# Softmax sums as 32-column products, four PE-summed units in the first block, and the skipped tiles' V added by VectorE

## The reference

```python
scores = einsum('bthd,bshd->bhts', q, k)          # 16 heads of 128
scores = scores * tril(ones((T, T)))              # masked scores are 0, not -inf
attn = softmax(scores / T ** 0.5, axis=-1)
out = einsum('bhts,bshd->bthd', attn, v).reshape(B, T, H * Dh) @ Wo
x = x + layernorm(out)
hdn = silu(g * gate_s) * (u * up_s)               # 5632 wide, from layernorm(x)
x = x + layernorm((hdn @ down_w.T) * down_s)
```

## Time and profile before

| | us |
|---|---|
| median of 3 runs | 3783.23 |
| lowest, highest | 3782.91, 4057.18 |
| the profiled execution | 3785.3 |
| its longest span, core 7 (odd) | 3783.8 |
| spans of the odd cores 1, 3, 5, 7 | 3778.8, 3769.3, 3779.7, 3783.8 |
| spans of the even cores 0, 2, 4, 6 | 3709.4, 3714.5, 3705.3, 3709.6 |
| busy on core 7: TensorE, VectorE, ScalarE, GpSimd | 3685.2, 1424.9, 1158.5, 173.1 |

### The profile page before, as it was taken

One profiled execution on the slowest core, in us unless ns is written; L12 is line 12 of the kernel. 1 busy time (PEld: TensorE's weight loads), 2 busy tenths in 40 slices (PEclk: granted clock), 3 DMA queues, 4 the chain that ended last, 5 costly groups with the idle time before them and its releaser, 6 DMA issues.

```text
span 3783.8 us, 50455 instructions; the slowest of 8 cores (3705.3 to 3783.8 us)
## 1 busy us (share of the span) xinstructions
PE 3685.2 (97%) x19252; PEld 1840.7 (49%) x19252; DVE 1424.9 (38%) x1860; ACT 1158.5 (31%) x1511; POOL 173.1 (5%) x235
## 2 busy tenths in 40 slices
PE   6999889999999999999999999999999999999998
PEld 3554444444454555545544444444444456645654
DVE  4641001101389999999976611102111121111112
ACT  2330000000288888888863310000010001101100
POOL 0000000000010000100000000000200001002000
PEclk9999989999999999999999999999999999999999
DMA  7534767798544335353036564554745547666665
GB/s 197 173 123 105 117 124 129 125 134 131 84 62 94 92 78 112 77 106 82 29 134 222 176 209 156 183 173 111 239 156 184 178 145 273 232 212 222 235 201 178
DMA packets 140788, 566.57 MB, mean 150 GB/s; under 512 B 38016, under 2 KB 83200, under 8 KB 111360
## 3 DMA queue, kind: packets, MB, share of 16 engines
q1 hardware_dynamic: 59520, 381.70, 29.6%
q0 software_dynamic: 11440, 125.83, 20.5%
q10 hardware_dynamic: 69584, 55.72, 4.9%
HBM read 595.73 MB, written 147.85 MB: 197 GB/s over the span
## 4 chain that ended last, share of the span: by engine, by line
PE 94%; ACT 2%; DMA 1%; issue 1%; ACTq 1%; DVE 1%; another core or an unknown queue 0%; DVEq 0%; POOL 0%; POOLq 0%; SPq 0%
PE ps L335 93%; ACT pt L369 1%; PE ps L340 1%; ACTq L331 1%; DMA xst<-x 0%; DMA indf<-ind 0%; DVE bna L361 0%; DVE zad L358 0%; ACT rz L369 0%; DMA kscr<-stg 0%; ACT xy L369 0%; DVE xy L360 0%; ACT zst L368 0%; DVE xn L359 0%
## 5 line engine op out<-in xcount | busy, mean ns | idle before, releaser
L335 PE MATMUL ps<-zt,slab 128*128 128x512 bf16 (+1 forms) x5632 | 1069.0, 353 | 6.2 <-DVE xy L360 6.2
L335 PEld LDWEIGHTS ps<-zt,slab 128*128 128x128 bf16 x5632 | 551.7, 98 | 522.4 <-issue 9.9
L369 ACT ACTIVATE pt<-ps 128x1024 bf16<-128x1024 f32 (+2 forms) x752 | 724.9, 981 | 132.9 <-PE ps L335 103.5
L358 DVE TENSOR_TENSOR zad<-zad,pt 128x1024 f32<-128x1024 f32 (+5 forms) x640 | 614.6, 975 | 59.5 <-POOL pt L364 2.9
L335 PE MATMUL ps<-dp,hall 128*128 128x512 bf16 x2332 | 504.0, 379 | 0.0
L360 DVE SCALAR_TENSOR_TENSOR hall<-ps,us_sb,sg 128x512 bf16<-128x512 f32 (+1 forms) x176 | 120.3, 684 | 902.6 <-PE ps L335 902.6
L335 PE MATMUL ps<-qh,kh 128*128 128x512 bf16 (+1 forms) x1760 | 432.4, 339 | 9.8 <-ACT qh L368 5.8
L335 PE MATMUL ps<-pt,vh 128*128 128x512 bf16 (+1 forms) x1760 | 432.3, 339 | 1.8 <-ACT pt L369 1.1
L369 ACT ACTIVATE sg<-ps,gs_sb 128x512 f32<-128x512 f32 (+1 forms) x176 | 111.2, 635 | 878.1 <-PE ps L335 878.0
L357 DVE CAST stg<-ps 128x512 bf16<-128x512 f32 (+1 forms) x136 | 89.7, 660 | 743.0 <-PE ps L335 707.4
L335 PEld LDWEIGHTS ps<-dp,hall 128*128 128x128 bf16 x2332 | 228.2, 98 | 274.9
(11 more groups left out here) (80 smaller groups left out, 1904.8 us busy)
## 6 DMA issues: line engine op xcount, KB each, us to landing
slab<-gwc SPq DMA_DIRECT2D x44, 2048.0 KB, 8.7
slab<-uwc SPq DMA_DIRECT2D x44, 2048.0 KB, 9.5
dp<-dwc SPq DMA_DIRECT2D x165, 512.0 KB, 4.8
xst<-x SPq DMA_DIRECT2D x32, 1024.0 KB, 5.8
gwc<-gw POOLq DMA_DIRECT2D x11, 2048.0 KB, 21.7
uwc<-uw POOLq DMA_DIRECT2D x11, 2048.0 KB, 19.5
dwc<-dw POOLq DMA_DIRECT2D x8, 2816.0 KB, 22.2
kh<-kscr SPq DMA_DIRECT2D x16, 1024.0 KB, 20.0
```

Of the source, the lines that this page charges most:

```text
L335: return c.r.op("tensor", lambda E: E.matmul(out, lhsT, rhs, start=start, stop=stop), waits=waits, inc="pe" if inc else None)
L358: "tt": lambda E, o, a, b, op: E.tensor_tensor(o, a, b, op),
L369: "act": lambda E, o, i, f, **kw: E.activation(o, i, f, **kw),
```

## The change

- Odd side, phase B: `npe` is 4, 4, 4, 2 instead of 2, 3, 3, 2, and `lag` is 5 for every block instead of 3. The TensorE sums of a block are no longer made unit by unit but in one burst after the block's last product with V (`zcols`): eight products with a 128 x 32 matrix of 1/32, each into one of four groups of 32 PSUM partitions, so that each group holds a quarter of the sum. VectorE adds the bank to its folded sum (`zr`), and splits that (`split`, now a few steps after `combine`); `zbc` opens the bank anew.
- Odd side: the product for the skipped tiles' V goes. 16 small products at the start of phase B give `vskip`, one value per row and query tile, and `mul` scales each tile of 128 columns by (output + vskip) x rz, 14 instructions a head instead of 4.
- Both sides: in group 1 each odd chunk of both loops makes a cast; the two casts at the group's end go. The order of the casts and their number stay.
- Both sides: `r.split()` stands before the first statistics, after the first wv load.
- Both sides: the first gate and up groups of phase C use the banks in another order: first the two that the last row tile of phase W didn't use.

```diff
-            self.npe = {18: 2, 22: 3, 26: 3, 30: 2}
-            self.lag = {18: 3, 22: 3, 26: 3, 30: 3}
+            self.npe = {18: 4, 22: 4, 26: 4, 30: 2}
+            self.cols = True
+            self.lag = {18: 5, 22: 5, 26: 5, 30: 5}
...
+    pop(c, "memset", c.ones32[:], 1.0 / 32.0)
...
+    ev_w["v0"] = dma(c, "gpsimd", "qw0", c.wres[0][:], d["wv"].ap()[0])
+    r.split()
+
     sop(c, "act", c.lva[1][:], c.eps[:], AF.Ln, waits=[ev_const])
 
-    ev_w["v0"] = dma(c, "gpsimd", "qw0", c.wres[0][:], d["wv"].ap()[0])
     def stats(t):
...
     apply(0)
-    r.split()
...
         ev_w[f"k{g}"] = dma(c, "gpsimd", "qw1", c.wres[1][:], d["wk"].ap()[g], waits=[r.mark("pe")])
         for cc in range(nch):
-            if g > 1 and cc % 2 == 1:
+            if cc % 2 == 1:
                 next_cast(c, [r.mark("pe")])
...
-            next_cast(c, [r.mark("pe")])
-            next_cast(c, [r.mark("pe")])
...
+    if sd.cols:
+
+        for h in range(H):
+            e = mm(c, bank(c, 6)[:, h * sd.n_own:(h + 1) * sd.n_own], c.vs[:, h * 128:(h + 1) * 128],
+                   c.ind[:, 0:sd.n_own], start=True, stop=True, waits=[c.ev_vs, c.ev_ind], inc=(h == H - 1))
+        ev_zbank = vop(c, "copy", c.vskip[:], bank(c, 6)[:, 0:H * sd.n_own], waits=[e] + c.ev_stores)
...
+            if not sd.cols:
+                mm(c, o[:, 0:W], c.vs[:, h * 128:(h + 1) * 128], skipped(n),
+                   start=True, stop=False, waits=w + [c.ev_vs, c.ev_ind])
...
+    def zcols(bi, us):
+
+        W = width[blocks[bi][1]]
+        parts = [(s, p[2]) for s in us for p in steps[s][4][0]]
+        assert len(parts) % 4 == 0
+        for i, (s, pc) in enumerate(parts):
+            j = i % 4
+            ev_zmm[s] = r.op("tensor", lambda E, j=j, s=s, pc=pc, i=i: E.matmul(
+                bank(c, 6)[32 * j:32 * j + 32, 0:W], c.ones32[:], c.pt[s % NPT][:, pc:pc + W],
+                start=(i < 4), stop=(i >= len(parts) - 4), tile_position=(0, 32 * j)),
+                waits=[ev_sel[s], ev_lnread[bi - 1] if bi >= 1 else ev_zbank],
+                inc="pe" if i == len(parts) - 1 or parts[i + 1][0] != s else None)
+
     def zbc(bi):
...
+    def split(bi):
+
+        W = width[blocks[bi][1]]
+        Z, e = c.zad, ev_fold[bi]
+        if sd.cols:
+            Z = c.zr
+            u = end_unit[bi]
+            e = vop(c, "tt", Z[:, 0:W], Z[:, 0:W], bank(c, 6)[:, 0:W], ALU.add, waits=[e, ev_zmm[u]])
...
+        if sd.cols:
+            for t in range(sd.blocks[n][1]):
+                x = h * sd.n_own + sd.blocks[n][0] - sd.own[0] + t
+                q = slice(t * 128, (t + 1) * 128)
+                ev_mul[bi] = vop(c, "stt", c.aall[:, a0 + t * 128:a0 + (t + 1) * 128],
+                                 bank(c, 4 + bi % 2)[:, q], c.vskip[:, x:x + 1], c.rz[:, q], ALU.add, ALU.mult,
+                                 waits=[ev_rz[bi], ev_last_pv[bi], c.ev_a_pe, ev_zbank])
+            return
...
+    plain = ([0, 1, 2, 3], [4, 5, 6, 7])
+    last = [c.ring(L, ds) for ds in range(4)]
+    free = [b for b in range(6) if b not in last]
+    first_banks = (free + last[:2], last[2:] + [6, 7])
```

More of the change, by code:

```diff
@@ L897, in pv @@
         o = bank(c, 4 + bi % 2)
+        w = []
         if k == 0:
             w = [ev_mul[bi - 2]] if bi >= 2 else [c.ev_ln1[1]]
-            mm(c, o[:, 0:W], c.vs[:, h * 128:(h + 1) * 128], skipped(n),
-               start=True, stop=False, waits=w + [c.ev_vs, c.ev_ind])
+            if not sd.cols:
+                mm(c, o[:, 0:W], c.vs[:, h * 128:(h + 1) * 128], skipped(n),
+                   start=True, stop=False, waits=w + [c.ev_vs, c.ev_ind])
         for m, (kt, c0, pc, pw) in enumerate(u[0]):
@@ L904, in pv @@
             ev_pvm[s] = mm(c, o[:, c0:c0 + pw], V[:, kt * 128:(kt + 1) * 128], P[:, pc:pc + pw],
-                           start=False, stop=(last and fin),
-                           waits=[ev_sel[s], ev_vl[h]] if m == 0 else (), inc=fin)
+                           start=(sd.cols and k == 0 and m == 0), stop=(last and fin),
+                           waits=w + [ev_sel[s], ev_vl[h]] if m == 0 else (), inc=fin)
         if last:
@@ L936, in zbc @@
         zb = bank(c, 6)[:, 0:W]
-        mm(c, zb, c.onesb[:], c.zhi[:, 0:W], start=False, stop=False, waits=[ev_zlo[bi]])
+        mm(c, zb, c.onesb[:], c.zhi[:, 0:W], start=sd.cols, stop=False, waits=[ev_zlo[bi]])
         ev_zbc[bi] = mm(c, zb, c.onesb[:], c.zlo[:, 0:W], start=False, stop=True, inc=True)
@@ L968, in combine @@
         while half >= W:
-            e = vop(c, "tt", Z[:, 0:half], Z[:, 0:half], Z[:, half:2 * half], ALU.add,
-                    waits=[r.mark("dve")])
+            o = c.zr if sd.cols and half == W else Z
+            w = [r.mark("dve")]
+            ev_fold[bi] = vop(c, "tt", o[:, 0:half], Z[:, 0:half], Z[:, half:2 * half], ALU.add, waits=w)
             half //= 2
+    def split(bi):
[5 more added lines that the diff above has]
+            e = vop(c, "tt", Z[:, 0:W], Z[:, 0:W], bank(c, 6)[:, 0:W], ALU.add, waits=[e, ev_zmm[u]])
         w = [e] + [ev_zbc[b] for b in (bi - 1, bi - 2) if b in ev_zbc]
@@ L995, in passes @@
         return sum(p[3] for p in steps[s][4][0]) / 512.0
-    mean = (sum(2 * passes(s) + (passes(s) if by_pe(s) else 0) for s in range(per_head))
+    share = 0.25 if sd.cols else 1.0
+    end_unit = {steps[s][0]: s for s in range(N)}
+    mean = (sum(2 * passes(s) + (share * passes(s) if by_pe(s) else 0) for s in range(per_head))
             + ND * sum(nt for t0, nt in sd.blocks) / 4.0) / per_head
@@ L1027, in phase_b @@
             if by_pe(p) and not all_pe[steps[p][2]]:
-                zmm(p)
-                work += passes(p)
+                if not sd.cols:
+                    zmm(p)
+                    work += passes(p)
+                elif steps[p][5]:
+                    b = steps[p][0]
+                    us = [q for q in range(p - 8, p + 1) if q >= 0 and steps[q][0] == b and by_pe(q)]
+                    zcols(b, us)
+                    work += share * sum(passes(q) for q in us)
         for p in z_at.get(s, ()):
@@ L1053, in phase_b @@
                 combine(steps[s][0])
+                if not sd.cols:
+                    split(steps[s][0])
+        for p in pv_at.get(s, ()):
+            if sd.cols and steps[p][5]:
+                split(steps[p][0])
     while c.casts:
@@ L1197, in phase_w @@
     c.NW = NW
+    c.ring = ring
     c.ev_w_pe = ev_mm[(NW - 1, 3)]
@@ L1324, in phase_c @@
             k = 2 * (b * NIG + ig)
+            gb, ub = first_banks if b == 0 and ig == 0 else plain
             for jj in range(4):
```

27 lines of the change are left out of this document (16 added, 11 removed).

## The result

| | before | after |
|---|---|---|
| median, us | 3788.57 | 3761.38 |
| ratio, 95% interval | | 0.9939 (0.9922 to 0.9956) |
| profiled execution, longest span | 3783.8 (core 7) | 3759.8 (cores 1 and 7) |
| spans of the odd cores 1, 3, 5, 7 | 3778.8, 3769.3, 3779.7, 3783.8 | 3759.8, 3759.5, 3754.7, 3759.8 |
| spans of the even cores 0, 2, 4, 6 | 3709.4, 3714.5, 3705.3, 3709.6 | 3702.8, 3702.9, 3698.3, 3690.6 |

Two of the five executions before and one of the five after ran slower as a whole at a lower granted clock, so the ratio compares the other three and four, whose medians are 3783.23 and 3761.28 us. The change wins 0.6%, 22 to 24 us, where 50 were forecast (3733 us), and lies 1.4 us above the upper end of the range. I compare core 7 with core 7.

What follows compares the result with a forecast made beforehand. VectorE and TensorE were taken as saturated in attention, odd core 7 slowest: 3785.3 − 5 (start) − 25 (casts) − 13 (attention) − 1.5 (its end) − 6 (FFN) = 3734.8, less 2.1 to the median: 3733 us; range 3715 to 3760.

Steps and rivals of the forecast that it cites:

- Attention: Odd side's heads: period falls from 58.8 to about 58.0 us, 13 us won over 16 heads (between −17 and +5).
- Waits of TensorE for the split: Attention: a listed sign that the forecast is wrong, TensorE waiting for VectorE's split; no size given.
- don't overlap: Rival, attention: 32-column products run one after another, TensorE needs 59.0 us a head, total 3751 us; chance 0.11.
- slow bursts: Rival, attention: weight loads can't hide, bursts cost 10.0 us a head, period 62.1, total 3799 us; chance 0.07.
- VectorE alone the bound: Attention: VectorE needs 57.8 us a head against TensorE's 54.4, so it alone sets the period of about 58.0.
- The casts: Group 1, odd cores: without the burst at 411 us, TensorE's 29.9 us stop becomes 5: −25 (−5 to −30).
- The remainder of 5: Group 1: a smaller burst from 277 to about 335 us still stops TensorE 0 to 10 us, taken as 5.
- the stall moves: Rival, group 1: the stop moves rather than goes, only 7 of 29.9 us is won, total 3751 us; chance 0.12.
- The penalty of 10 us by x: Even cores: a new cast at 174 us among the loads of x costs about 10 us, net −6.
- The start: Kernel start, both sides: the earlier branch hides part of VectorE's 8.6 us idle time: −5 us (0 to 9).
- The end of attention: Odd side: add and split after the last product take some 2.2 us instead of 3.7 of waiting: −1.5.
- The FFN's first group: FFN start: two banks free early let products cover the 6.2 us wait for VectorE: −6 on odd cores, 0 on even.

Runs made afterwards that it cites:

- e1: The changed kernel with lag 3 instead of 5 for block 26 alone: 3724.2 us.
- e8: e1 with the skipped tiles' V again a TensorE product and the scaling one instruction a block: 3744.2 us.
- e5: The kernel before with only the casts changed: one at each odd chunk of group 1's V loop, the two at the group's end gone: 3746.3 us.
- e12: e1 with one cast more in group 1, at the odd chunk of its K loop, right behind Wv: 3754.8 us.
- e13: The same kernel as e12, run again for its trace: 3752.8 us (one run).
- e11: e1 with the first FFN groups using the banks in the order of before: 3727.3 us.
- e2: The changed kernel with lag 3 instead of 5 for all four blocks: 3732.1 us.

## Why the prediction was wrong

**Attention, −13 forecast, +18 measured (core 7).** This is the step that failed: "The later scaling (lag 5) costs nothing as long as VectorE is less than five units late; what is queued behind a product that waits for its split is all of TensorE." I asked only who waits for the split. The scaling has a client too, the product with V that reuses the output's bank two blocks later, and the block between is 8 units long. The bound of five units was wrong: for block 26 the scaling stands two steps ahead of that product, behind the adds and folds of block 30, and VectorE came to it 1.5 us after rz was ready. The place in the list could have been read from the code. The wait costs 15 × 1.5 = 23, and the half clock behind 9 of them 9 × 1.7 = 15, which the forecast had nowhere: e1 measures 37 together. "Waits of TensorE for the split" was named as a sign of being wrong; the scaling was not.

**The prices of the operations held.** A burst of eight 32-column products takes 0.63 us, as priced. First its row in TensorE's timeline of after (core 7), then two groups by form (count, busy us, mean ns, idle before):

```profile
1532.44 0.61 PE L959 MATMUL ps<-pt,ones 128*32 128x512 bf16 x8
```

```profile
L370 DVE SCALAR_TENSOR_TENSOR aall<-ps,vskip,rz 128x128 bf16<-128x128 f32 x224 | 63.4, 343 | 1.9 <-ACT rz L379 1.9
...
L959 PEld LDWEIGHTS ps<-pt,ones 128*32 128x32 bf16 x512 | 7.7, 94 | 23.7 <-issue 23.7
```

Four scaling pieces take 1.23 us up to the next add (1577.61 to 1578.84; priced 1.08 and 0.1 of wait), one piece 0.343 (priced 0.35), and the add of the bank 0.78 (priced 0.79). The skip products are worth 1.6 us a head (e8 against e1; priced 1.55). The rivals "don't overlap" and "slow bursts" fall. The Trainium skill's page "TensorEngine Tiling (Array Packing)", sections "Key Properties" and "Restrictions and Gotchas", has a mode switch drain the engine and fast weight load off in column tiling; here a switch costs about 0.1 us each way within the 0.63, and the loads (94 ns each) stay hidden.

**"VectorE alone the bound" was wrong, and 58.0 close by luck.** With the lag mended the period is 57.53. TensorE's work was put at 54.4 and measures 55.4: 0.6 of it because before's sum (58.0) was short of its measured 58.64 busy, and I gave the difference to waiting; the rest is open. On top come the 2.0 us of waits for ScalarE in the TensorE-summed units. VectorE was put at 57.8 and needs 55.9 (57.5 less 1.6 of waits). I took VectorE's gapless row as a need of the whole head. The wait of 0.17 us in it stands ahead of all four splits of the head, 0.7 us where I took 0.3 off; the other 1.5 us are not accounted for.

**The casts, −25 forecast, some −38 measured alone (e5).** The mechanism was right, the size wrong in three ways. The remainder of 5 rested on a cast that isn't made; the wait for Q fell too (4.6), and the end of the half clock behind both stops gave 3 to 4 us more. And had the cast been made, the price of 0 to 10 us would have been wrong as well: "a store may be some 47 us late" holds at 411, where the tile is needed 47 us after the issue. At 272 it is needed after 20 us, and the stop was 25.7. The rival "the stall moves" was the true course for the kernel that I had in mind: of 29.9 us of stop 25.7 came back. Its 3751 isn't to be set beside e12, which has e1's lag.

**Even cores.** Their stop at 371 went, as forecast. The penalty of 10 us by x doesn't exist, as the cast isn't made; the net is −7 to −19 by core, and they never decide. With the cast made the price was about right: the even cores' spans average 3708.6 us in e12 against 3700.7 in e1, and core 6 of e13 waits 10.6 us for a staging tile from 196 on, where e1 waits 2.0.

**The start, −5 forecast.** The wait for Wv fell by 5.3, but the first normed tile came 5.8 later (17.2 to 22.9 us), which the wait hid. TensorE is 2.9 us ahead at the sixth tile (62.44 against 65.33). Over all traces that tile comes at 60.2 to 64.0 us with the early branch and at 65.3 to 67.4 with the late one: within the bounds.

**The end of attention, −1.5 forecast, +2.6.** The last split and scaling wait behind lag 5 too (6.28; 4.20 in e1). **The FFN's first group, −6 forecast**, −3 by e11: its wait is gone as forecast, but the transposes of the last row tile now wait 2.1 us for `zn` (3.1 in e1), which they don't in before, e5 or e11. A wait of 2.2 us at the sixth row tile is not the banks': e11 has it too, with 2.6.

For the version with one number mended, the forecast would be 3733 against 3724: there the attention gain (18 instead of 13) and the casts (38 instead of 25) outweigh the smaller start and banks (4 to 8 instead of 11). The range failed because it held no case in which the new order of VectorE's work makes TensorE wait in each head.

## What to carry to other kernels

When an instruction is moved later in its engine's list, list every buffer that it frees and count the steps to each next user, over the shortest block too: one of four equal-looking settings cost 1% here. Price a stop of TensorE with what follows it: up to 2 us more at the lower clock, here even behind 9 of 15 waits of 1.5 us. Spread big transfers so that no two are issued together ahead of a store whose buffer is needed soon, and compare the store's landing time with the time to the next use at that very place.

## What the runs showed of the hardware

- A wait of 1.51 us was followed by 4 us at a granted clock of 0.57 to 0.63 in 9 of 15 heads and at 1.00 in 6, with the same instructions (12 or 13 products in 4 us against 21). Behind e2's 15 waits of 1.5 to 1.9 us the clock was always 1.00. After waits of 25.7, 29.9 and 5.8 us it was 0.50; after the 1.25 us for Q in e5, 1.00. What decides, the runs don't tell.
- Four 32-column products on different column groups start 3 ns apart, and the next four 0.22 us later, so eight of 512 columns take 0.63 us with the changes of shape on both sides, against 0.43 for two ordinary ones; their weight loads of 94 ns are hidden.
- Independent VectorE instructions of three operands and 128 columns last 343 ns each but start 258 ns apart.
- A store of 256 KB on ScalarE's queue landed in 16.7 us beside one transfer of 2 MB on the software queue (e1) and in 44.9 us beside two issued within 0.6 us and a third 20 us later (e13).
